# Grouping the first norm and reordering the first and the last attention of a gated cross-attention block

## The reference

```python
def _L0_xattn_ref(q, latent_kv, Wq, Wkv_expand, Wout):     # H = 512, NH = 16 heads of 32
    qp = q @ Wq.T
    kv = latent_kv @ Wkv_expand.T
    k, v = jnp.split(kv, 2, axis=-1)
    ...
    scores = jnp.einsum('bhqd,bhkd->bhqk', qh, kh) * inv_sqrt_d
    causal = jnp.tril(jnp.ones((sq, sk), dtype=bool))
    scores = jnp.where(causal, scores, jnp.finfo(scores.dtype).min)
    attn = jax.nn.softmax(scores, axis=-1)
    out = jnp.einsum('bhqk,bhkd->bhqd', attn, vh)
    return out.transpose(0, 2, 1, 3).reshape(b, sq, H) @ Wout.T

def _L0_ffn_ref(x, gate_w, w1, w2, w3, ws1, ws2, ws3):     # 8 experts, the best 2 of each token
    scores = jax.nn.softmax(xf @ gate_w.T, axis=-1)
    weights, idx = jax.lax.top_k(scores, K)
    h = jnp.einsum('td,eid->eti', xf, w1)
    g = jax.nn.silu(h) * jnp.einsum('td,eid->eti', xf, w3)
    eo = jnp.einsum('eti,edi->etd', g, w2)
    comb = jnp.einsum('tke,tk->te', jax.nn.one_hot(idx, E, dtype=xf.dtype), weights)
    y = jnp.einsum('etd,te->td', eo, comb)
    z = jax.nn.silu(xf @ ws1.T) * (xf @ ws3.T) @ ws2.T     # the shared expert
    return (y + z).reshape(shape)

x = x + jnp.tanh(g_xattn[0]) * _L0_xattn_ref(_layernorm(x), ctx_512, Wq, Wkv_expand, Wout)
x = x + jnp.tanh(g_ffn[0]) * _L0_ffn_ref(_layernorm(x), gate_w, w1, w2, w3, ws1, ws2, ws3)
```

## Time and profile before

| | us |
|---|---|
| median of 3 runs | 450.63 (449.61 to 450.69) |
| the profiled execution | 452.13 |
| its span on the core | 450.4 |

### The profile page before, as it was taken

The page is one execution under the profiler, slowest core; times in us unless marked ns, Lnnn a source line. Parts: engine busy times, 40 slices in busy tenths (PEclk is TensorE's granted clock), DMA queues, the critical chain, the costliest instruction groups (busy, mean ns, idle before and its releaser), DMA issues.

```text
span 450.4 us, 8467 instructions
## 1 busy us (share of the span) xinstructions
PE 414.9 (92%) x2833; PEld 231.2 (51%) x2834; DVE 306.4 (68%) x663; ACT 239.3 (53%) x432; POOL 229.6 (51%) x206
## 2 busy tenths in 40 slices
PE   7989788999999999998987899999999999999980
PEld 7565445545546554464543455555555555555540
DVE  5989998888688876897869889844444444444430
ACT  2797784676647766855323448734344343434330
POOL 4019435636266762679343217565554646565422
PEclk9999999999999999998998999999999999999997
DMA  8940001706006075084343789575766666666543
GB/s 301 418 169 2 1 12 59 235 3 233 3 1 234 1 262 185 1 304 149 110 143 109 214 285 260 98 138 99 136 106 126 102 130 103 106 126 120 92 62 47
DMA packets 20769, 59.52 MB, mean 132 GB/s; under 512 B 3521, under 2 KB 3521, under 8 KB 20354
## 3 DMA queue, kind: packets, MB, share of 16 engines
q0 software_dynamic: 9504, 20.55, 25.4%
q1 hardware_dynamic: 11234, 38.56, 24.2%
HBM read 35.93 MB, written 23.17 MB: 131 GB/s over the span
## 4 chain that ended last, share of the span: by engine, by line
PE 61%; DVE 19%; POOL 7%; ACT 6%; issue 4%; another core or an unknown queue 1%; DMA 1%; POOLq 0%; DVEq 0%; ACTq 0%
PE bank L1671 46%; PE bank L1676 9%; DVE arena L1062 4%; POOL arena L590 3%; PE bank L1813 3%; POOL GT L615 2%; ACT arena L705 2%; DVE mv L1098 2%; DVE mx L1183 2%; ACT arena L753 1%; DVE xn L1152 1%; POOL ln L557 1%; PE bank L1824 1%; PE bank L1801 1%; DVE arena L1061 1%
## 5 line engine op out<-in xcount | busy, mean ns | idle before, releaser
L1671 PE MATMUL bank<-arena,GT 128*128 x468 | 107.4, 379 | 0.0
L689 POOL DMA_INDIRECT out<-rows,entry x39 | 62.7, 1609 | 65.9 <-issue 33.3
L1671 PE MATMUL bank<-arena,gT 128*128 (+1 forms) x336 | 80.2, 375 | 2.5 <-DVE x_sb L1282 1.3
L1671 PEld LDWEIGHTS bank<-arena,GT 128*128 128x128 f16 x468 | 45.8, 98 | 46.5
L705 ACT ACTIVATE arena<-bank 128x512 f16<-128x512 f32 (+1 forms) x88 | 48.5, 587 | 25.5 <-PE bank L1671 11.4
L666 POOL DMA_INDIRECT rows<-xrows,entry x39 | 38.9, 998 | 33.1 <-DVE entry L1462 11.3
L1062 DVE SCALAR_TENSOR_TENSOR arena<-bank,arena 128x512 f16<-128x512 f32 (+1 forms) x72 | 44.7, 663 | 12.4 <-ACT arena L705 7.5
L1671 PEld LDWEIGHTS bank<-arena,gT 128*128 128x128 f16 x336 | 32.5, 98 | 38.6 <-issue 3.2
L1061 DVE TENSOR_TENSOR gT<-bank,gT 128x256 f16<-128x256 f32 x55 | 23.0, 420 | 42.7 <-ACT gT L705 42.7
L1036 ACT ACTIVATE rows<-bank,weight 128x512 f32<-128x512 f32 x38 | 26.1, 687 | 38.0 <-PE bank L1671 38.0
L1627 DVE SCALAR_TENSOR_TENSOR uu<-th,bank 128x256 f32<-128x256 f32 x39 | 16.4, 421 | 43.4 <-ACT th L1003 42.8
(11 more groups left out here) (177 smaller groups left out, 675.2 us busy)
## 6 DMA issues: line engine op xcount, KB each, us to landing
x_sb<-in_experts SPq DMA_DIRECT2D x9, 768.0 KB, 6.1
rows<-in_experts SPq DMA_DIRECT2D x6, 768.0 KB, 6.3
xrows<-xn SPq DMA_DIRECT2D x16, 256.0 KB
out<-x_sb SPq DMA_DIRECT2D x16, 256.0 KB
image<-GT SPq DMA_DIRECT2D x5, 768.0 KB, 4.2
arena<-image SPq DMA_DIRECT2D x10, 384.0 KB, 4.0
x_sb<-in_x SPq DMA_DIRECT2D x1, 2048.0 KB, 16.8
x_sb<-in_x SPq DMA_DIRECT2D x2, 512.0 KB, 4.0
```

What stands on the lines that cost most here:

```text
L689: nc.gpsimd.indirect_dma_start(out=out, out_offset=bass.IndirectOffsetOnAxis(ap=entry[:, 1, j:j + 1], axis=0), in_=Y[:, j % RING, :], in_o ...
L1671: last = nc.tensor.matmul(dst, a, b, start=n == 0, stop=n == len(steps) - 1)
```

## The change

The first norm gets four groups instead of three: the four tiles of batch 0 are two groups of two, each with its aggregation and its power, and `first_norm` waits for the power of the group it is at. The GpSimd and VectorE calls with group numbers move up by one. `own_block` moves from ahead of the first norm to just ahead of the iteration of batch 0.

On ScalarE, `project_hi(0, 2)` comes ahead of `fill_k(0)`; in the iteration of batch 0 `exps(0, 0)` comes ahead of `scores_out(0, 3)`, and `exps(0, 2)` and `exps(0, 3)` have other places; `shared_hi_half(1)` comes ahead of `scores_out(1, 0)`.

On VectorE, `project_lo(0, 3)` and two turned tiles come ahead of `statistics1(8, 9)`; the head sums of batch 0 are spread in another way; `statistics1(11)` comes ahead of the mix, and those of tiles 12 to 15 come behind it instead of between its members; in the second norm of batch 0 `x1` comes ahead of `head_max`, and `aggregate2(0, 0)` ahead of `head_max(1, 1)`.

In the last attention, the groups of heads are taken in the order 2, 3, 0, 1 instead of 0, 2, 3, 1, and the four output products are written to banks in that order (`out_bank`). On VectorE all low parts of the probabilities come ahead of the logits and of `hidden(f, 2)`. On TensorE, three `keep_clock` matmuls stand where the wait for `hidden(f, 2)` stood; that wait is now ahead of group 0, and the one for `hidden(f, 3)` ahead of group 1.

```diff
-        ATTEND_LAST = (0, 2, 3, 1)
+        ATTEND_LAST = (2, 3, 0, 1)
...
+        def out_bank(b, i):
+
+            return mm_bank[ATTEND_LAST[i] if isinstance(b, int) and b == B - 1 else i]
...
-        LN1_GROUPS = ((0, PER), (PER, 2 * PER), (2 * PER, NT))
+        LN1_GROUPS = ((0, 2), (2, PER), (PER, 2 * PER), (2 * PER, NT))
...
             pool.wait_ge(consts, CONSTS)
             power1(0)
+            power1(1)
...
             def iteration(b, prev):
                 if prev is None:
+                    exps(b, 0)
                     scores_out(b, 3)
-                    exps(b, 0)
                     exps(b, 1)
+                    exps(b, 2)
                 else:
                     feed_forward(prev)
                 for kind, n in mix(b):
                     if kind == "q":
                         project_hi(b + 1, n)
-                        if prev is None and n < 2:
-                            exps(b, n + 2)
+                        if prev is None and n == 0:
+                            exps(b, 3)
...
-                scores_out(b + 1, 0)
                 if prev is None:
                     shared_hi_half(1)
+                scores_out(b + 1, 0)
                 scores_out(b + 1, 1)
...
+            project_hi(0, 2)
             fill_k(0)
-            project_hi(0, 2)
             project_hi(0, 3)
...
             def first_norm():
 
-                dve.wait_ge(ln1_power, 1)
                 for i in range(PER):
+                    dve.wait_ge(ln1_power, 1 + i // 2)
                     V.tensor_scalar(xn1[:, i * D:(i + 1) * D], x_tile(i), ln1[:, i, 0:1], ln1[:, i, 2:3],
                                     ALU.subtract, ALU.mult).then_inc(xn1_ready, 1)
...
-            dve.wait_ge(ld_x0[0], 16)
-            statistics1(range(2))
-            dve.wait_ge(ld_x0[1], 16)
-            statistics1(range(2, PER))
-            aggregate1(0)
-            own_block()
+            for n in range(2):
+                dve.wait_ge(ld_x0[n], 16)
+                statistics1(range(2 * n, 2 * n + 2))
+                aggregate1(n)
             first_norm()
...
                 head_sum(b, 2)
-                hidden(f, 2)
                 head_sum(b, 3)
-                router_logits(f)
                 for i in range(PER):
                     probabilities_lo(b, i)
+                router_logits(f)
+                hidden(f, 2)
                 hidden(f, 3)
...
             def iteration(b, prev):
                 if prev is None:
+                    head_sum(b, 0)
                     head_max(b, 3)
-                    head_sum(b, 0)
+                    head_sum(b, 1)
+                    statistics1(range(11, 12))
...
                         project_lo(b + 1, n)
                         if prev is None and n < 2:
-                            head_sum(b, n + 1)
+                            head_sum(b, n + 2)
                     elif kind == "v":
                         values_lo(n)
-                        if n == 0:
-                            head_sum(b, 3)
                     else:
                         probabilities_lo(b, n)
                         if prev is not None and n == 0:
                             head_sum(b, 3)
-                        if prev is None:
-                            statistics1(((11, 12), (13,), (14,), (15,))[n])
                 if prev is None:
-                    aggregate1(2)
+                    statistics1(range(12, NT))
+                    aggregate1(3)
...
-                head_max(b + 1, 0)
-                x1_and_statistics(b, 0)
-                if prev is None:
-                    bias1(2)
-                head_max(b + 1, 1)
-                x1_and_statistics(b, 1)
-                aggregate2(b, 0)
+                    x1_and_statistics(b, 0)
+                    head_max(b + 1, 0)
+                    bias1(3)
+                    x1_and_statistics(b, 1)
+                    aggregate2(b, 0)
+                    head_max(b + 1, 1)
+                else:
+                    head_max(b + 1, 0)
+                    x1_and_statistics(b, 0)
+                    head_max(b + 1, 1)
+                    x1_and_statistics(b, 1)
+                    aggregate2(b, 0)
                 norm2(b, 0)
...
+            project_lo(0, 3)
+            turn_lo(0, "x", 0)
+            turn_lo(0, "x", 1)
             dve.wait_ge(gates_ready, 2)
             dve.wait_ge(ld_x, 16)
             statistics1(range(8, 10))
-            project_lo(0, 3)
-            turn_lo(0, "x", 0)
-            turn_lo(0, "x", 1)
-            statistics1(range(10, 11))
             turn_lo(0, "x", 2)
             turn_lo(0, "x", 3)
-            for i in range(3):
-                head_max(0, i)
+            head_max(0, 0)
+            head_max(0, 1)
+            statistics1(range(10, 11))
+            head_max(0, 2)
+            own_block()
             iteration(0, None)
...
-                pe.wait_ge(g_ready, 4 * f + 3)
+                keep_clock(3, mm_bank[2])
                 split_done(b, "p", 2 * PER - 1)
                 for g in ATTEND_LAST:
                     if g == 3:
                         pe.wait_ge(lg_out, f + 1)
-                    if g == 1:
-                        pe.wait_ge(g_ready, 4 * f + 4)
+                    if g < 2:
+                        pe.wait_ge(g_ready, 4 * f + 3 + g)
                     attend(b, g).then_inc(a_mm, 1)
```

More of the change, by code:

```diff
@@ L627, in iteration @@
                 if prev is None:
-                    power1(2)
+                    power1(3)
                 else:
@@ L653, in last_iteration @@
                 scatter_pairs(prev, (1,))
-            power1(1)
+            power1(2)
             softmax_mask(0)
@@ L1129, in make_x1 @@
                 dve.wait_ge(y_mm, t + 1)
-                V.scalar_tensor_tensor(out=x_tile(t), in0=mm_bank[i][:, :], scalar=gl[:, 0:1], in1=x_tile(t),
+                V.scalar_tensor_tensor(out=x_tile(t), in0=out_bank(b, i)[:, :], scalar=gl[:, 0:1], in1=x_tile(t),
                                        op0=ALU.mult, op1=ALU.add).then_inc(x1_ready, 1)
@@ L1592, in _ @@
             statistics1(range(PER + 2, 2 * PER))
-            aggregate1(1)
+            aggregate1(2)
             project_lo(0, 1)
-            bias1(1)
+            bias1(2)
             keys_lo()
@@ L1823, in project_out @@
                     for u, v in ((0, 0), (0, 1), (1, 0)):
-                        last = nc.tensor.matmul(mm_bank[i][:, :], aTv[:, u, g, i * P:(i + 1) * P], woutv[:, v, g, :],
+                        last = nc.tensor.matmul(out_bank(b, i)[:, :], aTv[:, u, g, i * P:(i + 1) * P], woutv[:, v, g, :],
                                                 start=n == 0 and u + v == 0, stop=n == NG - 1 and u == 1)
```

## The result

The change is slower: 453.55 us median (452.0 to 453.7) against 450.63 (449.41 to 450.69), a ratio of 1.0062 with a 95% interval of 1.0038 to 1.0085. Forecast were 447.7, with a range of 446.0 to 450.3. The profiled execution of after takes 453.55 with a span of 451.8; that of before took 452.13 with 450.4.

The account below looks back on a forecast made before the run. TensorE was taken to bound the kernel, so only its stands or slow stretches pay. Batch 0's 1.1 plus the last attention's 1.85 made 2.95, taking the median from 450.63 to 447.7 us, range 446.0 to 450.3.

Parts of the forecast that it names:

- First norm: Batch 0's first norm in two groups: norms start at 8.05, 0.9 earlier; TensorE's first turn at 8.85, gaining 0.7.
- orders before the scores: New ScalarE and VectorE orders let TensorE score at 27.7 instead of 29.83; three score rounds end 1.3 earlier.
- own_block: Its instructions leave the shadow of the first norm's power for 36.5, costing VectorE 0.5 there.
- Softmax of batch 0: Later high and low projections delay values(0) to 42.3 from 41.93: the whole lead lost and 0.4 more.
- the stand: TensorE's wait ahead of values(0) in batch 0: 1.7 us, from projections done at 40.6 to values(0) at 42.3.
- The forecast gain of batch 0: Second norm's first turn at 72.75 instead of 73.85, so 1.1 handed on as a plain shift.
- (c): Rival: batch 0 gives nothing, the wait at values(0) being longer than 1.7; clock kept at the end, 448.8; chance 0.12.
- (d): Rival: slower, 452.7; clock falls ahead of values(0), before batch 0's attention and still in the last attention; chance 0.06.
- Last attention: At the kernel's end: clock kept, 48 matmuls in 2.75 instead of 4.46, project_out(0) 1.85 earlier; only 0.2 if it falls.
- The sum: Batch 0's 1.1 plus the last attention's 1.85 make 2.95, carried from the profiled execution to the median: 447.7.
- Rival (b): The shift also carries TensorE's 2.54 us wait at 237.8 out of its clock fall: 1.4 more, 446.3; chance 0.13.
- Rival (e): keep_clock delays the last attention instead of filling a wait, if low parts end 0.9 earlier; costs at most that.

Follow-up runs that it names:

- E1: Changed kernel with own_block moved to behind project_lo(0, 3), where VectorE waits and GpSimd is idle: 446.35 us against 449.33 for before, ratio 0.9951.
- E3: Kernel before with only the last-attention part of the change, three keep_clock matmuls included: 447.4 us against 449.33 for before, ratio 0.9972.
- E14: Kernel before with keep_clock matmuls in two TensorE waits, ahead of batch 0's attention and of count_pairs: 447.68 us against 448.15, ratio 0.9986.
- E2: Changed kernel with 11 keep_clock matmuls added ahead of values(0) on TensorE: 448.99 us against 449.33 for before, ratio 1.0005.
- E7: The changed kernel itself, run again on a second chip: 452.72 us against 450.84 for before there, ratio 1.0054.
- E10: E1 with the statistics of tiles 11 to 15 spread anew, four of them into VectorE's waits: 447.88 us against 450.84 for before, ratio 0.9936.
- E5: E3 without its three keep_clock matmuls: 450.34 us against 450.84 for before, ratio 0.9984.
- E6: Kernel before with only three keep_clock matmuls ahead of the wait before the last attention: 450.69 us against 450.84 for before, ratio 0.9992.
- E15: E14 with three keep_clock calls ahead of the last attention too: 447.62 us against 448.15 for before, ratio 0.9975.

## Why the prediction was wrong

**First norm, orders before the scores: right.** Norms at 7.95 (8.05 said), first turn at 8.55 (8.85), first scores at 27.51 (27.7).

**own_block: the step that failed.** The prediction says that it moves to 36.5, "where they cost VectorE 0.5". The duration was taken from a stretch in which GpSimd was idle until its short power started at 7.86, and put into one in which GpSimd subtracts without a pause. It measured 2.9. Timelines of GpSimd and VectorE, before, at the old place:

```profile
7.86 1.05 POOL L557 TENSOR_TENSOR ln<-ln,minus_half 128x4 f32<-128x4 f32 x1 [2.58 <-DVE ln L1109]
...
7.93 0.16 DVE L1070 SCALAR_TENSOR_TENSOR own<-own,down_no 128x1 f32<-128x1 f32 x1
```

The prediction had the rule of the Trainium skill (GPSIMD Engine Reference, section 8, Key points) in hand and did not ask it of the instructions that the change moves: it weighed the two halves of the shared expert and called the statistics free, rightly. In the form in which it was cited, two SBUF inputs, the rule covers the third instruction (1.76) but not the cast (1.10), which has one. The trace of before shows the case on a small instruction of bias1. Timelines of GpSimd and VectorE, before:

```profile
67.28 1.90 POOL L590 TENSOR_TENSOR arena<-arena,mx 128x1024 f32<-128x1024 f32 x1 [2.92 <-DVE mx L1177]
...
68.62 0.59 DVE L1124 SCALAR_TENSOR_TENSOR ln<-ln 128x8 f32<-128x8 f32 x1
```

It takes 0.59 where it otherwise takes 0.17, and ends at 69.2, when the subtraction ends.

**Softmax of batch 0: the mechanism right, the size from own_block.** With own_block away the stand is 0.92, not the 1.7 said: the projections ended at 41.0 and not at 40.6, and values(0) started at 41.96 and not at 42.3, without own_block's 0.5 ahead of it. From attention on the starts agree with the working within 0.2 us. The forecast gain of batch 0, 1.1, is E1 less E3 (446.35 and 447.4 on one chip). It became a loss of 3.0: 2.43 for the held instructions and 1.57 for the fall of the clock behind the stand that they stretched to 3.45, less a gain of 1.0. Rivals (c) and (d) name that place, (c) with the stand longer than 1.7 and (d) with the fall; the outcome is both at once, which no rival had. (d) priced a fall at 1.7, near the 1.57; (c) let batch 0 give nothing, and it lost 1.4 by the held instructions alone. Both at once had no chance of its own.

**Last attention: the mechanism right, its value too high.** The clock was kept, attention began 1.07 behind the passes (1.0 said), and between the two profiled executions 1.9 came out where 1.85 was said. But the sum was carried to the median as if every run had the fall. Only a part has it: the term is 0.2 and 1.65 times that part. On the chip of E14 this is an estimate of 0.2 + 0.4 (3 runs of 12); on that of E3 the ratio of 0.9972 is 1.25 us. Neither is 1.85. The prediction noted that the profiled execution of before lay 1.5 above the median and "carried the difference, not the absolute". That 1.5 was the warning: a profile with one fall more than the median run.

**The sum again.** Without any fall after would lie 1.2 behind before: 1.0 gained in batch 0, 2.43 lost there, 0.2 gained in the last attention (E2 measured +1.4 between the lowest steps). On E7's chip the falls of after add the rest to +3.7 in the median. There its runs have a mean clock of 0.983 to 0.990, those of before mostly 0.988: the median of before has one fall, that of after one to two. In the first pair six of the seven runs of after have 0.983 or 0.984, two falls as in its profile, and the median of before lies 1.5 below its profile with two, so it has one. That makes 1.2 and 1.6 for one fall more, 2.8; measured were 2.92. So the forecast failed twice: own_block's 0.5, and a sum that counted falls of the clock in one profile as if all runs had them and no new one would come.

**Rival (b)** saw that the wait at 238 matters, but took the fall there as something the shift would cure. After has it still. The profiles of before, after, E7 and E10 show it behind a wait of 2.5, those of E5 and E6 don't behind the same wait, and no profile shows it where the wait is 1.7. So what matters there is the length of the wait, which goes with the chip; that this fall comes and goes in one kernel is shown by no profile.

**Rival (e)** did not come: keep_clock ends 1.07 before attention.

## What to carry to other kernels

When an instruction is moved, take its duration from a row where the neighbours run what they run at the new place; on VectorE ask first what GpSimd does there. Read all runs of a kernel, not only the median: clusters 1.6 us apart with nothing between them mean a switch that flips in some runs, and a gain read from one profile counts only with the share of runs that have it. Matmuls of a constant in three of TensorE's waits took 0.25% (0.08 to 0.43) off before and narrowed its spread from 3.4 to 0.6 us, with no order changed; in E15 they ended 0.8 us or more before the data came in two of the waits, and filled the third.

## What the runs showed of the hardware

A VectorE instruction with two SBUF inputs, and a cast from SBUF to SBUF, don't only slow down beside GpSimd's subtractions: they end when the running one ends. 0.16 became 1.76, 0.22 became 1.10 to 1.59, beside subtractions of 1.87 each. Beside the short power at 7.86 in before the third instruction still took its 0.16. It goes the other way too: GpSimd's mask takes 1.15 alone, 1.92 in before and 2.38 in E1, each time ending 1.0 after the half of the shared expert that VectorE had started before it. A reduction of the same tile took 0.28 beside the subtractions, head_max 1.21, and statistics 0.68, as alone. The Trainium skill (Advanced Engine Details and Errata, "VectorE Performance Modes") says that GpSimd's instructions and VectorE's two-port ones interfere or block each other; the runs agree with "block", and give it a length: here up to one GpSimd subtraction for each VectorE instruction.

The clock of TensorE fell to 1.2 GHz behind waits of 1.5 to 3.5 us and came back; the same wait of 3.45 us, in the same kernel, was followed by a fall in one execution and by none in another. That the gate does not follow the kernel's start, as the Trainium skill has it (TensorE: Matmul & The Clock Gate, "What's actually happening"), agrees with this. What decides in which run a wait is hit was not tried, nor how short a wait is safe.
